# Edge MLP rows kept once in fp32, and the loop's weights formed by two 64-row fp32 products

## What is computed

```
for W in (W_mlp1, W_mlp2, W_mlp3):            # 8 -> 64 -> 64 -> 64
    h = SILU_2MOM * silu(h @ W / sqrt(W.shape[0]))
tpw = h @ W_mlp4 / sqrt(64)                   # 64 -> 512
w1, w2, w3, w4 = jnp.split(tpw, 4, axis=-1)
s0 = x0[sender];  s1 = x1[sender]             # 128 and 3 x 128 features
p1 = w1 * s0 * y0                             # and p2, p3, p4 in the same way
msg = segment_sum(messages, receiver)
```

## Time and profile before

| | us |
|---|---|
| median of 3 runs (lowest to highest) | 2420.47 (2417.71 to 2429.76) |
| the profiled execution, whole | 2428.48 |
| its span in the trace | 2426.5 |
| MLP stage, first Silu to the end of the last | 184.1 to 270.9 |
| first product of the loop's weights | 284.1 |
| last scatter of the loop | 964 |

### The profile page before, as it was taken

One profiled execution on the slowest core, in us unless ns is written; L12 is line 12 of the kernel. 1 busy time (PEld: TensorE's weight loads), 2 busy tenths in 40 slices (PEclk: granted clock), 3 DMA queues, 4 the chain that ended last, 5 costly groups with the idle time before them and its releaser, 6 DMA issues.

```text
span 2426.5 us, 44871 instructions
## 1 busy us (share of the span) xinstructions
PE 2170.3 (89%) x13390; PEld 1528.1 (63%) x13391; DVE 1344.2 (55%) x2859; ACT 1005.6 (41%) x2267; POOL 644.0 (27%) x761
## 2 busy tenths in 40 slices
PE   6999588888888877879999999999699999979998
PEld 4544255445545544858888888888464564558886
DVE  2325388888888877555565556555700126273444
ACT  3008233333333332227777777777231002344443
POOL 3002377777777777330000000002200000000000
PEclk9999789999999999859999999999899999989999
DMA  8608667676767766755440440032600000220000
GB/s 206 194 5 270 212 190 194 186 191 193 193 187 199 194 185 193 301 189 208 182 164 17 156 156 26 17 129 86 224 1 13 35 35 0 70 70 1 18 9 17
DMA packets 196602, 310.31 MB, mean 128 GB/s; under 512 B 55047, under 2 KB 121285, under 8 KB 192008
## 3 DMA queue, kind: packets, MB, share of 16 engines
q1 hardware_dynamic: 149574, 177.59, 22.4%
q0 software_dynamic: 38928, 125.00, 17.9%
q10 hardware_dynamic: 8034, 6.84, 0.8%
HBM read 247.13 MB, written 63.55 MB: 128 GB/s over the span
## 4 chain that ended last, share of the span: by engine, by line
PE 61%; issue 12%; DVE 9%; DMA 5%; POOL 4%; ACT 3%; another core or an unknown queue 2%; DVEq 1%; POOLq 1%; ACTq 1%; SPq 0%
PE psum L2239 13%; PE psum L2368 6%; PE psum L2401 4%; PE psum L2283 4%; PE psum L2229 3%; DMA xn_T<-sender_table,wide 3%; PE psum L2230 3%; PE psum L2231 3%; PE psum L2312 3%; PE psum L2301 3%; POOL xn_T L953 3%; PE psum L2275 3%; PE psum L1958 2%; PE psum L2091 2%
## 5 line engine op out<-in xcount | busy, mean ns | idle before, releaser
L953 POOL DMA_INDIRECT xn_T<-sender_table,wide x372 | 382.3, 1028 | 164.3 <-issue 89.0
L2091 PE MATMUL psum<-big_b,wide 128*32 128x256 f32 (+2 forms) x3680 | 291.6, 402 | 12.4 <-POOL wide L978 11.2
L2239 PEld LDWEIGHTS psum<-xn_T,big_b 128*128 128x128 f32 x2048 | 261.9, 191 | 21.2 <-issue 3.2
L2091 PEld LDWEIGHTS psum<-big_b,wide 128*32 128x32 f32 x3680 | 175.8, 112 | 147.3 <-issue 62.2
L2239 PE MATMUL psum<-xn_T,big_b 128*128 128x128 f32 x2048 | 265.0, 275 | 0.0
L2058 PE MATMUL psum<-w_hi,h_slot 128*128 128x512 f32 x372 | 171.1, 460 | 87.9 <-DVE big_b L1549 55.8
L1147 ACT ACTIVATE wide<-psum 128x384 f32<-128x384 f32 x45 | 22.1, 492 | 432.3 <-PE psum L2102 253.0
L1547 DVE TENSOR_TENSOR big_b<-psum,xn_T 128x512 f32<-128x512 f32 x184 | 126.9, 690 | 121.6 <-DMA xn_T<-sender_table,wide 105.8
L1722 DVE TENSOR_TENSOR w_lo<-wide,w_hi 128x512 fp32r<-128x512 f32 x184 | 127.4, 692 | 120.1 <-ACT w_hi L1238 116.0
L2229 PE MATMUL psum<-w_hi,hid_hi 128*128 128x512 f32 x368 | 175.5, 477 | 12.9 <-DVE w_lo L1722 7.2
L1549 DVE TENSOR_TENSOR big_b<-xn_T,psum 128x768 f32<-128x768 f32 x184 | 174.1, 946 | 0.0
(11 more groups left out here) (395 smaller groups left out, 3973.4 us busy)
## 6 DMA issues: line engine op xcount, KB each, us to landing
big_a<-in_L_ffn_W SPq DMA_DIRECT2D x12, 2048.0 KB, 13.9
big_b<-in_L_ffn_W SPq DMA_DIRECT2D x12, 2048.0 KB, 13.8
h_slot<-edge_hidden SPq DMA_DIRECT2D x186, 128.0 KB
edge_hidden<-h_parts SPq DMA_DIRECT2D x42, 512.0 KB
wide<-in_L_ffn_W SPq DMA_DIRECT2D x8, 2048.0 KB, 23.6
tokens_sorted<-zeros SPq DMA_DIRECT2D x2, 3712.0 KB, 27.2
adj_dram<-big_a SPq DMA_DIRECT2D x1, 6400.0 KB, 29.1
xn_T<-tokens_sorted POOLq DMA_DIRECT2D x25, 256.0 KB, 2.9
```

What stands on the lines that cost most here:

```text
L953: nc.gpsimd.indirect_dma_start(out=sent[q][:, j, :], out_offset=None, in_=sender_table, in_offset=bass.IndirectOffsetOnAxis(ap=indices[j], ...
L2091: nc.tensor.matmul(msg_psum[k].rearrange("p (c u) -> p c u", u=MUL)[bands[g], cols, :], hot_y[q][:, j, y, :], p[:, of, :], start=False, st ...
L2239: last = nc.tensor.matmul(psum[:, f % UP_BANKS, 0:P], ew1[a][:, c, f * P:f * P + P], tile_T[:, c, :], start=(c == 0), stop=(c == C - 1))
```

## The change

The hidden rows are no longer split. SP stores `h3_out` itself, once, as fp32 (one DMA a turn instead of two, half of the bytes), as soon as the third Silu is done. DVE's two operations per turn and the split of `w_mlp4` are gone, with their semaphores. ACT's third Silu now waits until the store of three turns before has landed, where it waited for the split. `edge_hidden` is half as large, and the loop's load brings one 128x128 fp32 tile, 64 KB instead of 128 KB: partitions 0 to 63 hold the hidden rows of the edges j = 0, partitions 64 to 127 those of j = 1. `tile_weights` is one fp32 product per j, of 64 rows, in its own half of the array's rows, each into its own PSUM bank as before. `w_mlp4` lies in both halves of the partitions already.

```diff
-        edge_hidden = dram("edge_hidden", (2, J // 2, 2, HID, XPAD))
+        edge_hidden = dram("edge_hidden", (J // 2, 2, HID, XPAD))
...
-            h3_slot = [sb_r(f"h3_slot{q}", [P, 2, P]) for q in range(HALVES)]
-            w4_hi = sb_r("w4_hi", [P, 4 * MUL])
-            w4_lo = sb_r("w4_lo", [P, 4 * MUL])
...
+        h3_slot = [wide[:, H3_OUT + q * P:H3_OUT + (q + 1) * P] for q in range(HALVES)]
...
-            hidden_cols = edge_hidden.rearrange("h q t c x -> h c (q t) x")
+            hidden_cols = edge_hidden.rearrange("q h c x -> (h c) q x")
             for n in range(TURNS):
                 a = n % RING
-                sp.wait_ge(h3_split, n + 1)
-                for h in range(2):
-                    sp.dma_start(hidden_cols[h, :, :, n * TURN_UNITS * P:(n + 1) * TURN_UNITS * P],
-                                 h3_parts[h * HID:(h + 1) * HID, a, :, :, :].rearrange("p q t x -> p (q t) x").bitcast(F32))\
-                        .then_inc(h3_stored[a], 16)
+                sp.wait_ge(silu_done[2], n + 1)
+                sp.dma_start(hidden_cols[:, :, n * TURN_UNITS * P:(n + 1) * TURN_UNITS * P], h3_out[a])\
+                    .then_inc(h3_stored[a], 16)
 
             def hidden_load(q, s, x):
                 sp.wait_ge(weights_done, s * 4 + q + 1)
                 sp.sem_inc(loop_entered, 1)
-                sp.dma_start(h3_slot[q][:, :, :].bitcast(F32),
-                             edge_hidden[:, q % 2, :, :, x].rearrange("h t c x -> (t c) h x"))\
+                sp.dma_start(h3_slot[q], edge_hidden[q % 2, :, :, x].rearrange("h c x -> (h c) x"))\
                     .then_inc(half_loaded[q], 16)
...
                 if layer == 2:
                     dst = h3_out[n % RING]
                     if n >= RING:
-                        act.wait_ge(h3_split, n - RING + 1)
+                        act.wait_ge(h3_stored[n % RING], n // RING * 16)
...
-            settle(nc.vector.tensor_copy(w4_hi[:, :], w_mlp4[:, :]))
-            nc.vector.tensor_tensor(w4_lo[:, :], w_mlp4[:, :], w4_hi[:, :].bitcast(F32), ALU.subtract).then_inc(w4_ready, 1)
...
-                dve.wait_ge(silu_done[2], n + 1)
-                if n >= RING:
-                    dve.wait_ge(h3_stored[a], n // RING * 32)
-                nc.vector.tensor_copy(h3_parts[:, a, :, 0, :], h3_out[a]).then_inc(hi_ready, 1)
-                dve.wait_ge(hi_ready, n + 1)
-                nc.vector.tensor_tensor(h3_parts[:, a, :, 1, :], h3_out[a], h3_parts[:, a, :, 0, :].bitcast(F32), ALU.subtract)\
-                    .then_inc(h3_split, 1)
...
             def tile_weights(q):
                 for j in range(2):
-                    nc.tensor.matmul(tile_w[q % 2][:, j, :], h3_slot[q][:, j, :], w4_hi[:, :], start=True, stop=False)
-                    last = nc.tensor.matmul(tile_w[q % 2][:, j, :], h3_slot[q][:, j, :], w4_lo[:, :], start=False, stop=True)
+                    last = nc.tensor.matmul(tile_w[q % 2][:, j, :], h3_slot[q][halves[j], :], w_mlp4[halves[j], :], start=True, stop=True)
                 last.then_inc(weights_done, 1)
```

More of the change, by code:

```diff
@@ L137, in graph_block_kernel @@
             z2_hi = overlay.enter_context(nc.sbuf_tensor("z2_hi", [P, NT, D], F32R))
-        with ExitStack() as overlay:
-            h3_parts = overlay.enter_context(nc.sbuf_tensor("h3_parts", [P, RING, 2, 2, TURN_UNITS * P], F32R))
         big_b = sb("big_b", [P, NT * NP])
@@ L152, in graph_block_kernel @@
             H3_OUT = RING * 2 * TURN_UNITS * P
-            sb_r("ahead_of_slots", [P, H3_OUT])
-            h3_slot = [sb_r(f"h3_slot{q}", [P, 2, P]) for q in range(HALVES)]
-            w4_hi = sb_r("w4_hi", [P, 4 * MUL])
-            w4_lo = sb_r("w4_lo", [P, 4 * MUL])
-            OVERLAY = H3_OUT + HALVES * 2 * P + 2 * 4 * MUL
+            OVERLAY = H3_OUT + 4 * D
             W2_HI = A["L0_ffn_W1"].shape[2] // P // 2 * D
-            sb_r("ahead_of_w2", [P, 2 * W2_HI - OVERLAY])
+            sb_r("ahead_of_w2", [P, 2 * W2_HI])
             w2_hi = sb_r("w2_hi", [P, 2, D])
@@ L320, in graph_block_kernel @@
         first_records_loaded = sem("first_records_loaded")
-        h3_split = sem("h3_split")
         half_loaded = [sem(f"half_loaded{q}") for q in range(HALVES)]
-        w4_ready = sem("w4_ready")
-        hi_ready = sem("hi_ready")
         record_loaded = [sem(f"record_loaded{q}") for q in range(HALVES)]
@@ L758, in _ @@
             for a in range(RING):
-                sp.wait_ge(h3_stored[a], len(range(a, TURNS, RING)) * 32)
+                sp.wait_ge(h3_stored[a], len(range(a, TURNS, RING)) * 16)
             step = step_counter(sp, "sp_step")
@@ L1115, in _ @@
             act.wait_ge(span_ready, 1)
-            act.wait_ge(h3_split, TURNS)
             act.sem_inc(step_ready, 8)
@@ L1480, in _ @@
                 nc.vector.tensor_tensor(x_rows[:, t, :], full, x_rows[:, t, :], ALU.add).then_inc(free, 1)
-            dve.wait_ge(loads["mlp"], 16 * (TURN_UNITS * J + 8))
-            settle(nc.vector.tensor_copy(w4_hi[:, :], w_mlp4[:, :]))
-            nc.vector.tensor_tensor(w4_lo[:, :], w_mlp4[:, :], w4_hi[:, :].bitcast(F32), ALU.subtract).then_inc(w4_ready, 1)
             def edge_inputs(n):
@@ L1490, in edge_inputs @@
                 nc.vector.tensor_copy(ea_T[n % RING], ea_bank(n)).then_inc(ea_T_ready, 1)
-            def split_hidden(n):
-                a = n % RING
-                dve.wait_ge(silu_done[2], n + 1)
-                if n >= RING:
-                    dve.wait_ge(h3_stored[a], n // RING * 32)
-                nc.vector.tensor_copy(h3_parts[:, a, :, 0, :], h3_out[a]).then_inc(hi_ready, 1)
-                dve.wait_ge(hi_ready, n + 1)
-                nc.vector.tensor_tensor(h3_parts[:, a, :, 1, :], h3_out[a], h3_parts[:, a, :, 0, :].bitcast(F32), ALU.subtract)\
-                    .then_inc(h3_split, 1)
             dve.sem_inc(hot_low_ready, 8)
@@ L1504, in _ @@
             edge_inputs(0)
[L1505 to L1513, removed]
+            for n in range(1, TURNS):
+                edge_inputs(n)
             dve.wait_ge(records_stored, 16)
@@ L2065, in _ @@
             pe.wait_ge(span_ready, 1)
-            pe.wait_ge(w4_ready, 1)
             for q in range(2):
```

## The result

The changed kernel takes 2412.77 us in the median, the kernel before 2425.07 us in runs beside it: a ratio of 0.9953 (95% interval 0.9942 to 0.9965), 12.3 us or 0.47% less. Measured again on another chip the ratio was 0.9962 (0.9941 to 0.9982). The forecast was 18 us less, from 2420.5 to 2402.5, with a range of 2382 to 2420. Sign and range held; a third of the gain is missing, and what is there came from other places than forecast.

The account below looks back on a forecast made before the run. It took PE and ACT, then transfers, to bound the MLP stage, and a ring of POOL, gather and DVE the loop. Savings of 8 + 5.9 + 0 + 0 + 4 = 18 us from 2420.5 gave 2402.5, range 2382 to 2420.

Parts of the forecast that it names:

- Part 1: End of the MLP stage: halved stores remove most of a 13 us stall; 8 us saved, bounds 0 and 13.
- second rival: MLP stage: the stall belongs to the gathers, which stay; only 6 to 8 us saved, 2413 us; chance 0.2.
- late releases: MLP stage: DVE waited 5.88 us and ACT 4.86 us for something remote, long after the matmuls that should release them.
- 257.8 us: MLP stage: where the last third Silu should end at 3.32 us a round, against 270.9 in the trace.
- Part 2: From last Silu to the loop's first hidden load: 4.9 us instead of 10.8; gain 5.9, bounds 4 and 7.
- Part 3: DVE in the MLP stage: the removed split, 21 times 1.9 us, and two weight operations are worth nothing by themselves.
- Part 4: PE in the loop: weights group 1.0 to 1.1 us against 1.12; counted as 0, bounds -7 to +5.
- series rival: PE in the loop: row halves run in series, 0.76 us more per quarter, about +60 us, 2466; chance 0.04.
- Part 5: Transfers in the loop: halved hidden loads let gathers land sooner; 4 us saved, bounds 0 and 16.
- first rival: All waiting was for DMA: stall 13, tail 7, loop 12, together 32 us saved, 2388 us; chance 0.2.
- the line of 0.5%: Whole kernel: about 12 us, what a measurement can tell from no change; the line lies at 2408.4 us.
- "same": Whole kernel: the outcome of no distinguishable change, chance 0.22, beside faster 0.70 and slower 0.08.

Follow-up runs that it names:

- one_row_half: The changed kernel with both fp32 products of a quarter in rows 0 to 63 of the array: 2476.62 us, ratio 1.0269 to the kernel before.
- the doubled load: The changed kernel with each hidden load back at 128 KB, in 256 pieces, half of it used: 2421.22 us, against 2410.61 us for the changed kernel.
- the pair with held gathers: Changed kernel and kernel before, each with the first twelve gathers held until the last turn's third Silu is done: 2397.08 and 2401.41 us.
- late_gathers: The changed kernel with POOL's first twelve gathers held until the last turn's third Silu is done: 2397.08 us, ratio 0.9950 to the kernel before.
- small_gathers: The changed kernel with the first eight gathers bringing 32 bytes of each row instead of 2 KB: 2401.84 us, ratio 0.9953 to the kernel before.
- four_gathers: The changed kernel with the first eight gathers made direct 32-byte copies, four staying indirect: 2391.38 us, ratio 0.9908 to the kernel before.
- four_again: The changed kernel with the first eight gathers made direct copies, four indirect in a close row, on another chip: 2388.39 us, ratio 0.9914 to the kernel before.
- four_spaced: The changed kernel with eight gathers made direct copies, the other four each issued after the one before landed: 2387.57 us, ratio 0.9928 to the kernel before.
- four_held: The changed kernel with eight gathers made direct copies, the other four held until the last third Silu: 2404.60 us, ratio 0.9915 to the kernel before.

## Why the prediction was right and where it was wrong

**Part 1, the stall, was wrong: 8 us forecast, none came.** The step that failed is "most, because DMA saturation goes". The share of 0.99 in the stall was read as its cause. It was a companion: the share was the same 0.99 from 195 to 239 us, where nothing stalled, as the second rival said. The forecast had looked at 190 to 242 us, whose 0.91 hides this, as its start lies ahead of the stores' full rate. What began at 240 us was the issuing of indirect gathers in a close row, and the late releases named in Part 1 were the whole of it, with PE's own pauses and its lower clock behind them, not a remainder of 5 us. Held gathers (257.6 and 259.0 us) show the cause, small gathers and full DMA rule the bytes out, fills rule a busy POOL out, and spacing (259.7 and 258.8 us) shows that the close row matters. "It is wrong if the last Silu still ends at 268 or later" was the sign named for this, and it came. The 257.8 us that were extrapolated for a stage without the stall were right.

**Part 2, the tail, was right**: 4.85 us forecast as 4.9, with the load to PE 0.25 us shorter. Its price for the store, 1.53 us, came from the queue's rate in the stage itself. Only the sum is confirmed, not its split into 1.53 and 3.4. The section of the Trainium skill that the prediction names there (DMA: Bandwidth & Descriptors, Anatomy of one DMA) gives its figure for DMAs issued by POOL. Here a store of 512 KB issued by SP landed 2.7 us after its issue in the median of 195 to 239 us of the changed kernel, against the 3.2 us of that estimate.

**Part 3, the removed DVE work, was right** at nothing. ACT's new wait for a store of three turns before never shows among its waits.

**Part 4, PE, was right**: 1.06 us for a forecast of 1.0 to 1.1, row halves side by side, mode change included. The series rival priced itself at 0.76 us a quarter and 60 us; one_row_half measured 0.85 us and 66 us, so the rival's price was well placed too. No run separates the drain that the skill names.

**Part 5, the halved loads, was probably under-sized**: 4 us taken, 10.6 by the medians of the doubled load, about 1 by the pair with held gathers, all inside the bounds of 0 and 16. The sum of the changed kernel speaks for more than 4: its first products start 3.9 us earlier than before (282.3 and 286.2 us), and the medians differ by 12.3, which leaves 8 for the loop. If so, the term that was mis-sized is the choice between the bounds, "the load lies beside a gather only part of the time". (The hidden loads are 23.5 MB, 179 times 128 KB, not 22.9; it changes nothing.)

**The sum.** By the sizes in the two traces 0 + 5.9 + 0 + 0 + 8 = 14, less 2.3 for the later end of the stage, is 12, close to the 12.3 of the medians; that the 8 fits so well is partly luck, by what was said of single traces. The forecast of 18 was 5.7 us too high: 8 from Part 1 that didn't come and 2.3 lost, against 4 or more from Part 5. Of the rivals, the second had the mechanism of the stage right ("they stay, so only the tail and a little more is saved") and the time (2413) almost to the microsecond. That is luck: it forecast 6 to 8 us less, where 12.3 came, and the kernel before took 2425.07 us in these runs, not the 2420.5 that it counted from. The first rival failed at its stall. The forecast lay beyond the line of 0.5%; the 0.47% measured lies on the side of "same", which had a chance of 0.22, and its interval (0.35% to 0.58%) holds the line.

**Open.** Why close indirect gathers delay the others isn't shown. The late releases, and PE's transposes 0.7 us each with nothing to wait for, look like engines that are late at fetching or signalling rather than at computing, which is a guess. Loads of program code are no slower, at least: the DMA view of 238 to 272 us shows the same line for the changed kernel, with the stall, and for late_gathers, without it:

```profile
q8 instruction: 2, 0.03, 0.4%
```

In the loop gathers come in pairs all the time, and the two PE groups shown take as long as before (1.06 and 1.12 us, 1.50 and 1.49); whether its straight-line code makes the MLP stage sensitive, or the row of twelve, was not tried. Nor is it shown what sets the loop's rhythm of short and long blocks: the loops of the changed kernel (twice), small_gathers, four_gathers, four_again, four_spaced and four_held, whose loop code is the same and whose first products wait for no gather, span 661.9 to 679.3 us.

## What to carry to other kernels

A full resource beside a stall is not yet its cause: look for a stretch in which the same resource is as full and nothing stalls, and for what starts at the moment the stall starts, then remove that alone. Indirect DMAs that only fill slots or run ahead can be made direct or spaced out when other engines work beside them. A 64-row fp32 product in each row half of the array cost no more here than the four products of a split. And a difference of 8 us between two single traces of a loop is no finding where traces of one and the same loop differ by 17; pairs of many runs are needed, and two such pairs may still disagree.

## What was not expected of the hardware

- Twelve indirect DMAs of 128 rows, issued every 1.3 us, delayed PE, ACT and DVE by 13 to 15 us in all, with ACT idle 7.59 us ahead of a Silu where 0.37 us is usual, and did so when eight of them brought 32-byte rows, at a DMA share of 0.45. Issued 4.3 us or more apart, three or four beside the stage cost at most 2 us. Eight direct DMAs from POOL in 4.24 us left ACT's round at 3.33 us.
- DMA at 0.99 for 16 us, with 1 MB of stores every 3.3 us, left PE at 14.59 of 16 us.
- Two fp32 products of 64 rows and 512 columns in the two row halves take 1.06 us, and 1.91 us in one half.
